# Scan stage of a two-layer metaformer: where ScalarE's steps stand between the recurrence steps, and which engine forms the last sum

## The chip, the cores and the metric

The kernel runs on one core of a Trainium2 chip. The metric is the device time of one launch in microseconds. The profile names the engines PE (TensorE, with PEld for its weight loads), DVE (VectorE), ACT (ScalarE), POOL (GpSimd) and SP (SyncE, which here only issues DMAs). All data is fp32.

## The reference, cut to what matters

Input x is 64 images of 56 x 56 tokens with 128 channels. Layer 0 is a window attention and a recurrent network, layer 1 a state-space convolution and a mixture of experts. The change touches the stage that holds layer 0's recurrence and layer 1's convolution:

```python
# layer 0, second half: 3136 dependent steps for all 64 images
yt = sigmoid(wx_t + yt @ Vt)
t = t + ys                                   # residual: input of layer 1
# layer 1, first half, per token of n = layernorm(t)
fg = sigmoid(n @ Wf + bf + 2); ig = sigmoid(n @ Wi + bi); delta = softplus(n @ Wd + bd) * 0.1
inp = delta * ig * (B * n)                   # complex product, B from a DFT of 7 x 7 taps
for _ in range(16):                          # h_r, h_i
    h = fg * (A * h) + inp                   # done in closed form, by repeated squaring
x3 = t + h                                   # the last sum of residual and convolution
```

## The kernel before, in words

`scan_phase` (lines 623 to 1265) is written with an explicit program for each engine and semaphores between them. Tokens are taken in NCH = 25 chunks of TF = 128 (the last has 64), images in NO = 4 groups of OS = 16. `slots()` (L744) yields pairs (j, s) of chunk and group. In one slot three things run side by side, each for another group:

* the recurrence of chunk j: K = 32 steps k. At each, PE multiplies the last state by `vh` (L1236) and ACT takes the tanh (L1107). PE then has to wait for ACT and ACT for PE, so every further instruction that either engine is given stands, in program order, between two steps.
* the front half for group `oc`: PE turns the states back to token-major and adds the input (`turn_u`, L1194: two 512-column passes of `ident` on `X2` and eight short ones), ACT evacuates this into `X2` (`residual`, L1073), DVE takes statistics (L910), POOL the inverse root (L832 to L836), ACT normalizes into `XN` (L1123), PE turns it (`turn_normal`, L1219), ACT evacuates it (L1142), and PE and ACT make 16 gates (L1265, L1084, L1086). At the slot's end ACT runs an Exp and a Ln over the whole group (L1164, L1166), each after a table load.
* the back half for group `o = oc - 1`: DVE's chain of products L986 to L1043, with seven squares by ACT in between (L1128 to L1157). DVE counts its steps in the semaphore `dv` (NV = 24 a group), ACT its squares in `am` (NA = 7). The last two DVE instructions are L1041 (half the sum of `Wv` and `IN`) and L1043 (`X2` added, result in `IN`), and SP stores `IN` (L794).

PE also turns the next chunk's inputs (`turn_inputs`, L1207) into bank `pX`, and ACT copies them to `XU` (`keep_turned`, L1061), with the state order changed in that copy: it reads 512 contiguous values and writes each to a place 256 bytes from the one before. Every eighth step PE adds `inputs` (L1191, 512 columns). `turn_u` for the next group stands at k = 24, 26, 28 and 30, except in slot s = 3; for s = 0 it stands at k = 0 to 3 of its own slot. The order of work is written out by hand: each engine's loop over k has the places in `if` conditions. Nothing is planned by a program.

SP loads `X2` of group o+1 (L781) once `dv` says that the group two before is finished, as there are NX = 3 buffers. The slot order on SP is load, DFT rows, store.

Of the kernel before, what the change touches and what calls it, by code (L numbers as in the profile page):

```python
# [14 lines left out]
ALU = mybir.AluOpType  # L15
# [607 lines left out]
def scan_phase(nc, B, x1_d, xh_d, gram, w_ffnT, v_ffnT, gamma, beta, w_gates, b_gates, dft, kernA, kernB,  # L623
# [7 lines left out]
    OS = 16  # L631
# [3 lines left out]
    NX = 3  # L635
# [6 lines left out]
    NV = 24  # L642
# [18 lines left out]
    with ExitStack() as ctx:  # L661
# [68 lines left out]
        dv = sem("dv"); am = sem("am")  # L730
# [13 lines left out]
        def slots():  # L744


            for j in range(-1, NCH + 2):
                for s in range(NO):
                    g = (j - 1) * NO + s
                    if g <= NGR:  # L750
                        yield (j, s, g if 0 <= g < NGR else None, g - 1 if 1 <= g else None,
                               0 <= j < NCH, j + 1 < NCH)
# [10 lines left out]
        def _(sp):  # L763
# [20 lines left out]
            for j, s, oc, o, scan, prep in slots():  # L784
                if oc is not None and oc + 1 < NGR:
                    load_x1(oc + 1)
# [4 lines left out]
                if o is not None:  # L791
                    c, s_ = divmod(o, NO)
                    sp.wait_ge(dv, o * NV + NV)
                    sp.dma_start(tokens(x3_d, OS * s_, OS, c),  # L794
                                 IN[0:size(c)].rearrange("t r b c -> t (r b c)").rearrange("t (b c) -> t b c", b=OS)
                                 ).then_inc(x3_st, 16)
# [3 lines left out]
        def _(pool):  # L800
# [14 lines left out]
            for j, s, oc, o, scan, prep in slots():  # L815
# [28 lines left out]
        def _(dve):  # L844
# [114 lines left out]
            for j, s, oc, o, scan, prep in slots():  # L959
# [6 lines left out]
                if o is not None:  # L966
# [32 lines left out]
                    wait(dve, x3_st, o * 16)  # L999
# [3 lines left out]
                if o is not None:  # L1003
                    after(7)
                    turned_by(tm, Wv, inp, a, wp_d, wv_d, o)
                    dve.wait_ge(am, o * NA + 3)
# [9 lines left out]
                if o is not None:  # L1016
                    dve.wait_ge(am, o * NA + 5)
# [3 lines left out]
                    did(dve.scalar_tensor_tensor(f1[:, 1], t1, -1.0, d1, ALU.add, ALU.mult))  # L1021
                    did(dve.scalar_tensor_tensor(f0[:, 0], f0[:, 0], -0.25, d0, ALU.add, ALU.add))
                    did(dve.scalar_tensor_tensor(t0, t0, 1.0, d0, ALU.add, ALU.mult))
                    dve.wait_ge(am, o * NA + 6)
# [25 lines left out]
        def _(act):  # L1050
# [10 lines left out]
            def keep_turned(j, s, q):  # L1061
# [5 lines left out]
                if j >= 1:  # L1067
                    act.wait_ge(y_ps, i - 2 * NO * NQ + 1)
                act.copy(XU[n % 2][:, 0:size(n), b0:b0 + Q].rearrange("c t b -> c b t"),
                         pX[:, 0:Q * size(n)].rearrange("c (b t) -> c b t", b=Q)).then_inc(xt_sb, 1)  # L1070
                load_xq(i + 2)

            def residual(oc, q):  # L1073
# [3 lines left out]
                act.copy(X2[oc % NX][0:tc, Q * q:Q * q + Q, :].rearrange("t b c -> t (b c)"), pY[0:tc, :]).then_inc(x2_d, 1)  # L1077

# [12 lines left out]
            for j, s, oc, o, scan, prep in slots():  # L1091
# [11 lines left out]
                for k in range(K):  # L1103
# [7 lines left out]
                    if conv and s + 1 < NO and k in (25, 27, 29, 31):  # L1111
                        residual(oc + 1, (k - 25) // 2)
                    if prep and k in (1, 4, 7, 10):
                        keep_turned(j, s, k // 3)
                    if conv and 10 <= k < 10 + NQ:
                        q = k - 10
                        if q == 0:
# [4 lines left out]
                        for i in range(Q * q, Q * q + Q):  # L1122
                            w = act.activation(XN[0:tc, i, :], X2[oc % NX][0:tc, i, :], ACT.Identity,  # L1123
                                               bias=nmr[0:tc, i:i + 1], scale=rst[0:tc, i:i + 1])
                        w.then_inc(xn_d, 1)
                    if o is not None and k == 6:
                        needs(4)
                        act.activation(t1, t0, ACT.Square).then_inc(am, 1)  # L1128
                        act.activation(f0[:, 0], t0, ACT.Square, bias=cols[0:tm, 1:2]).then_inc(am, 1)
                    if o is not None and k == 8:  # L1130
                        act.activation(d1, d0, ACT.Square).then_inc(am, 1)
                    if o is not None and k == 14:
                        act.wait_ge(am, o * NA + 3)
                        act.activation(d2, d1, ACT.Square).then_inc(am, 1)
                    if scan and s == NO - 2 and k == 25:
                        act.wait_ge(mag_d, j + 1)
                        act.activation(sc_[0:size(j)], sa[0:size(j)], ACT.Tanh, scale=0.5).then_inc(th_d, 1)
                    if conv and 12 <= k < 12 + NQ:
                        q = k - 12
# [7 lines left out]
                    if o is not None and k == 16:  # L1147
                        needs(8)
                        act.activation(t2, t1, ACT.Square).then_inc(am, 1)
                    if o is not None and k == 20:  # L1150
                        if conv:
                            act.wait_ge(bx_d, oc + 1)
                        act.activation(f1[:, 0], t1, ACT.Square, bias=cols[0:tm, 2:3]).then_inc(am, 1)
                    if o is not None and k == 22:
                        needs(11)
                        act.wait_ge(am, o * NA + 6)
                        act.activation(t1, t2, ACT.Square, bias=cols[0:tm, 2:3]).then_inc(am, 1)  # L1157
# [11 lines left out]
        def _(pe):  # L1169
# [36 lines left out]

            def turn_inputs(j, s, q, oc):  # L1207
# [7 lines left out]
                for b in range(Q):  # L1215
                    w = pe.transpose(pX[:, tn * b:tn * b + tn], XQ[i % 2][0:tn, b, :], ident[0:tn, 0:tn])
# [9 lines left out]
            for j, s, oc, o, scan, prep in slots():  # L1226
# [4 lines left out]
                for k in range(K):  # L1231
# [17 lines left out]
                    if conv and s + 1 < NO and k in (24, 26, 28, 30):  # L1249
                        turn_u(oc + 1, (k - 24) // 2)  # L1250
                    if prep and k in (0, 3, 6, 9):
                        turn_inputs(j, s, k // 3, oc)
                    if conv and 11 <= k < 11 + NQ:
                        if k == 11:
                            if scan and s == NO - 2:
                                pe.wait_ge(raw_d, j + 1)
                            if prep:
                                pe.wait_ge(xt_sb, ((j + 1) * NO + s) * NQ + NQ)
                        turn_normal(oc, tc, k - 11)
# [552 lines left out]
```

## Time and profile before

| | us |
|---|---|
| median of 3 runs | 14605.63 |
| lowest, highest | 14566.55, 14616.49 |
| the profiled execution, its span | 14537.58, 14535.8 |
| Exp of the first and of the last of 100 groups in the scan stage, start | 5509.7, 11648.4 |

The page also gives the busy share of the whole span: PE 79%, PEld 60%, DVE 76%, ACT 68%, POOL 28%. These are means over all stages. For this change only the stretch between the two Exp instructions matters, where DVE's digit in the 40 slices is 9 throughout and the granted TensorE clock is 6 to 7 tenths. A time in the rows is the start from the span's beginning, and the next number the duration of the group of instructions. An instruction's duration overlaps the next one's on the same engine, so what it costs in a queue is the distance from its start to the next start.

### The profile page before, as it was taken

What the parts mean: (1) busy time and instruction counts of PE and PEld (TensorE: products, weight loads), DVE (VectorE), ACT (ScalarE), POOL (GpSimd) and SP (SyncE); (2) the same over time, 40 slices, a digit from 0 to 9 for tenths busy, and PEclk for the clock granted to TensorE, in tenths of its full rate; (3) what the DMA queues carried; (4) which work ended last, traced back from release to release, by engine and by line L of the source; (5) the groups of instructions that cost most, each with busy time, mean ns of one, the idle gap of its engine ahead of it and who ended that gap; (6) DMA issues with size and microseconds to landing.
All of it is one profiled execution on the core that took longest, in us unless ns stands there. A gap on an engine that the chain in (4) does not pass through costs nothing. (4 is left out here: it accounts for less than half of the span.)

```text
span 14535.8 us, 248087 instructions
## 1 busy us (share of the span) xinstructions
PE 11419.5 (79%) x87538; PEld 8744.4 (60%) x87538; DVE 11053.6 (76%) x22880; ACT 9833.3 (68%) x22679; POOL 4012.8 (28%) x3975
## 2 busy tenths in 40 slices
PE   7888888888888867777777777777777547776998
PEld 5666666666666645555555555555555235555888
DVE  6777777777777718999999999999999965554133
ACT  6888888888888846666666666667666567776100
POOL 5444444445444421212111211112121111211000
PEclk9999999999999967777777777777777677777555
DMA  3333333333333321111111111111111133333599
GB/s 69 86 81 82 81 82 87 76 90 73 90 77 86 75 61 41 53 53 53 51 47 52 53 53 53 51 46 53 53 52 40 23 84 94 99 90 89 172 316 309
DMA packets 1967708, 1189.72 MB, mean 82 GB/s; under 512 B 48853, under 2 KB 1900056, under 8 KB 1958436
## 3 DMA queue, kind: packets, MB, share of 16 engines
q1 hardware_dynamic: 1554148, 967.87, 26.3%
q10 hardware_dynamic: 408832, 205.55, 5.0%
q8 instruction: 641, 10.50, 0.3%
q14 instruction: 439, 3.60, 0.1%
q0 software_dynamic: 3648, 2.20, 0.1%
HBM read 708.85 MB, written 466.62 MB: 81 GB/s over the span
## 5 line engine op out<-in xcount | busy, mean ns | idle before, releaser
L1236 PEld LDWEIGHTS s_pW<-s_XU,s_vh 128*128 128x128 f32 x6272 | 1415.7, 261 | 1969.1 <-ACT s_XU L1107 1699.7
L1236 PE MATMUL s_pW<-s_XU,s_vh 128*128 128x64 f32 x6272 | 1493.2, 331 | 1071.4 <-ACT s_XU L1107 1071.4
L1107 ACT ACTIVATE s_XU<-s_pW,s_zb 128x64 f32<-128x64 f32 x3136 | 995.7, 318 | 1788.7 <-PE s_pW L1236 1738.1
L1265 PE MATMUL s_pG<-s_wg,s_XNT 128*128 128x384 f32 (+1 forms) x3200 | 1506.0, 559 | 37.5 <-ACT s_Z L1086 37.5
L832 POOL TENSOR_TENSOR s_rst<-s_var,s_epst 128x16 f32<-128x16 f32 (+1 forms) x100 | 141.7, 1417 | 3906.6 <-DVE s_var L79 3906.6
L408 ACT ACTIVATE KB<-pV,qkb 32x392 f32<-32x392 f32 x2048 | 1190.5, 581 | 25.0 <-PE pV L498 1.1
L248 POOL TENSOR_TENSOR SS<-SS,mx 128x784 f32<-128x784 f32 x512 | 769.5, 1503 | 804.8 <-DVE mx L341 804.6
L1203 PEld LDWEIGHTS s_pY<-s_hident,s_XU 128*128 128x128 f32 (+1 forms) x3200 | 752.2, 305 | 177.7 <-issue 129.6
L1711 PE MATMUL c_pS<-c_OX,c_Wm 64*112 64x128 f32 x3584 | 737.6, 420 | 91.1 <-DVE c_X L1727 76.6
L460 ACT ACTIVATE XH<-XR,nm,rs 112x128 f32<-112x128 f32 x1792 | 733.6, 485 | 92.1 <-POOL nm L267 83.6
L506 PE MATMUL pS<-KB,QT 128*64 128x196 f32 x8192 | 793.7, 336 | 0.0
L1711 PEld LDWEIGHTS c_pS<-c_OX,c_Wm 64*112 64x112 f32 x3584 | 728.2, 304 | 100.5 <-DVE c_X L1727 85.7
L1123 ACT ACTIVATE s_f<-s_X,s_nmr,s_rst 128x128 f32<-128x128 f32 (+1 forms) x1600 | 658.0, 492 | 162.0 <-POOL s_nmr L836 161.9
L528 PE MATMUL pV<-wq,XT 128*49 128x64 f32 x16384 | 565.7, 222 | 251.0 <-ACT KB L408 250.7
L1453 ACT ACTIVATE r_Y<-r_X,r_nmr,r_rst 112x128 f32<-112x128 f32 x1792 | 718.7, 508 | 56.6 <-POOL r_nmr L1395 56.6
L506 PEld LDWEIGHTS pS<-KB,QT 128*64 128x64 f32 x8192 | 544.9, 137 | 352.6 <-issue 284.9
L256 POOL TENSOR_TENSOR XR<-XR,pbias 112x512 f32<-112x512 f32 x448 | 571.6, 1276 | 650.9 <-DMA XR<-in_x_dram 650.9
L352 DVE RECIPROCAL rc<-pO 128x16 f32<-128x16 f32 x512 | 131.3, 256 | 796.9 <-PE pO L549 796.9
L549 PE MATMUL pO<-Vb,PT 128*64 128x66 f32 x16384 | 591.1, 225 | 169.3 <-DVE gram L346 165.6
L1203 PE MATMUL s_pY<-s_hident,s_XU 128*128 128x128 f32 (+1 forms) x3200 | 716.8, 369 | 0.0
L528 PEld LDWEIGHTS pV<-wq,XT 128*49 128x49 f32 x16384 | 490.1, 124 | 371.4 <-ACT KB L408 370.9
L1727 DVE TENSOR_TENSOR c_X<-c_pS,c_X 112x512 f32<-112x512 f32 x448 | 307.4, 691 | 521.6 <-PE c_pS L1711 391.4
(249 smaller groups left out, 31958.3 us busy)
## 6 DMA issues: line engine op xcount, KB each, us to landing
XL<-in_x_dram SPq DMA_DIRECT2D x64, 1568.0 KB, 12.4
XR<-in_x_dram SPq DMA_DIRECT2D x64, 1568.0 KB, 18.0
x_dram<-XR SPq DMA_DIRECT2D x64, 1568.0 KB, 8.1
xh_dram<-XH SPq DMA_DIRECT2D x64, 1568.0 KB, 8.1
r_X<-x_dram SPq DMA_DIRECT2D x64, 1568.0 KB, 14.2
c_X<-x_dram SPq DMA_DIRECT2D x64, 1568.0 KB, 19.4
out_dram<-c_X ACTq DMA_DIRECT2D x64, 1568.0 KB, 13.9
s_XQ<-xh_dram ACTq DMA_DIRECT2D x384, 256.0 KB, 2.8
```

Of the source, the lines that this page charges most:

```text
L248: pool.tensor_tensor(sv[:], sv[:], mx[wi % 2][:].unsqueeze(2).broadcast_to([P, 16, L]), ALU.subtract).then_inc(s_sub, 1)
L408: i = act.activation(KB[par][r, :, h, :], pV[r, 0:NW * L].rearrange("c (w l) -> c w l", l=L), ACT.Identity, bias=qkb[r, 1:2])
L460: i = act.activation(XH[q.par][:, n0, 0:C], XR[q.par][:, n0, :], ACT.Identity, bias=nm2[:, k, t:t + 1], scale=rs2[:, k, t:t + 1])
L506: i = pe.matmul(pS[64 * s:64 * s + 64, p // 2, (p % 2) * NH * L:(p % 2 + 1) * NH * L], QT[par][:, w * L:w * L + 64], KB[par][:, w, :, :].r ...
L528: i = pe.matmul(pV[64 * o:64 * o + L, 64 * w:64 * w + 64], XT[im.par][:, wi, w, :], wq[:, 2 * C:3 * C].rearrange("c (a b d) -> c a b d", a ...
L1107: act.activation(XU[j % 2][:, t, :], pW[t // R % 2][:, B * (t % R):B * (t % R) + B], ACT.Tanh, bias=zb[:, 0:1], scale=0.5).then_inc(u_sb, 1)
L1123: w = act.activation(XN[0:tc, i, :], X2[oc % NX][0:tc, i, :], ACT.Identity, bias=nmr[0:tc, i:i + 1], scale=rst[0:tc, i:i + 1])
L1203: w = pe.matmul(pY[0:tc, C * i:C * i + C], XU[c % 2][:, 0:tc, OS * s + Q * q + i], hident[:], start=False, stop=True, skip_group_check=True)
L1236: pe.matmul(pW[t // R % 2][:, B * (t % R):B * (t % R) + B], vh[:], before, start=False, stop=True, skip_group_check=True).then_inc(z_ps, 1)
L1265: pe.matmul(pG[i % 3][0:tc, 0:3 * C], XNT[:, i, 0:tc], wg[:], start=True, stop=True).then_inc(g_ps, 1)
L1453: w = act.activation(Y[m.par][o][:, t, :], X[m.par][o][:, t, :], ACT.Identity, bias=nmr[m.par][o][:, t:t + 1], scale=rst[m.par][o][:, t:t ...
L1711: w = pe.matmul(bank[0:T, C * t:C * t + C], Wm[m.par][E * o:E * o + E, T * n:T * n + T], OX[m.par][E * o:E * o + E, :], start=True, stop=True)
```

## The change

1. The last sum. DVE's L1041 becomes a plain sum of `Wv` and `IN`, L1043 goes, NV is 23. In the next slot PE adds `X2` and `Wv` in bank `pN` (`last_sum`, two matmuls of 512 columns by `ident`, a quarter of the group at k = 1, 3, 5 and 7), and ACT evacuates each quarter into `X2` at k = 2, 4, 6 and 8, with the constant 0.5 as bias. SP stores `X2` after ACT's four, and only then reloads that buffer for the group three later; in the slot the load stands last now.
2. ACT's places. The normalization runs two rows at a step over eight steps from k = 7 (k = 11 for s = 0), where it ran four at a step over four steps from k = 10. The evacuations that follow come at every second step. The squares move from k = 6, 6, 8, 14, 16, 20, 22 to 6, 15, 17, 19, 21, 22, 24, in another order, and DVE's waits on `am` are renumbered. The residual's turn moves to k = 17, 19, 21, 24, its copies to 18, 20, 22, 25. The inputs' turns are at 0, 2, 4, 7, their copies at 1, 3, 5, 8.
3. The inputs' order. `turn_inputs` writes `pX` with a step of four values, and `keep_turned` reads it contiguously and writes four adjacent values at a time.

```diff
-    NV = 24
+    NV = 23
+        TURN_IN = (0, 2, 4, 7)
+        KEEP_IN = (1, 3, 5, 8)
+        TURN_U = (17, 19, 21, 24)
+        KEEP_U = (18, 20, 22, 25)
+        def normal_at(s):
+            return 11 if s == 0 else 7
...
             def load_x1(o):
-                wait(sp, dv, (o - NX + 1) * NV)
+                wait(sp, x3_st, (o - NX + 1) * 16)
...
+                    sp.wait_ge(f_sb, f * NQ + NQ)
+                    sp.dma_start(tokens(x3_d, OS * s_, OS, c), X2[f % NX][0:size(c)]).then_inc(x3_st, 16)
+                if oc is not None and oc + 1 < NGR:
+                    load_x1(oc + 1)
...
+                    wait(dve, f_ps, o * NQ)
                     turned_by(tm, Wv, inp, a, wp_d, wv_d, o)
...
-                    did(dve.scalar_tensor_tensor(flat(wv), flat(wv), 0.5, flat(inp), ALU.add, ALU.add))
-                    after(23)
-                    did(dve.tensor_tensor(flat(inp).rearrange("t (b r c) -> t b r c", b=OS, r=2),
-                                          X2[o % NX][0:tm].rearrange("t b (r c) -> t b r c", r=2),
-                                          wv.rearrange("t r b c -> t b r c"), ALU.add))
+                    did(dve.tensor_tensor(flat(wv), flat(wv), flat(inp), ALU.add))
...
-                act.copy(XU[n % 2][:, 0:size(n), b0:b0 + Q].rearrange("c t b -> c b t"),
-                         pX[:, 0:Q * size(n)].rearrange("c (b t) -> c b t", b=Q)).then_inc(xt_sb, 1)
+                act.copy(XU[n % 2][:, 0:size(n), b0:b0 + Q],
+                         pX[:, 0:Q * size(n)].rearrange("c (t b) -> c t b", b=Q)).then_inc(xt_sb, 1)
...
+            def last_sum(f, q):                                   # ACT
+                act.wait_ge(f_ps, f * NQ + q + 1)
+                act.activation(X2[f % NX][0:tf_, Q * q:Q * q + Q, :]..., pN[0:tf_, :],
+                               ACT.Identity, bias=cols[0:tf_, 1:2]).then_inc(f_sb, 1)
...
-                    if conv and 10 <= k < 10 + NQ:                # normalization, 4 rows at a step
+                    i = 2 * (k - normal_at(s))
+                    if conv and 0 <= i < OS:                      # 2 rows at a step
...
-                    if conv and 12 <= k < 12 + NQ:                # evacuation of the turned rows
+                    if conv and k - normal_at(s) - 3 in (0, 2, 4, 6):
...
+                        if k == 24:
+                            needs(11)
+                            act.wait_ge(am, o * NA + 5)
+                            act.activation(t1, t2, ACT.Square, bias=cols[0:tm, 2:3]).then_inc(am, 1)
...
+            def last_sum(f, q):                                   # PE
+                wait(pe, f_sb, f * NQ + q)
+                pe.matmul(pN[0:tf_, :], ident[0:tf_, 0:tf_], X2[f % NX][0:tf_, Q * q:Q * q + Q, :]..., start=True, stop=False)
+                pe.matmul(pN[0:tf_, :], ident[0:tf_, 0:tf_], Wv[0:tf_, :, Q * q:Q * q + Q, :]..., start=False, stop=True
+                          ).then_inc(f_ps, 1)
...
-                    w = pe.transpose(pX[:, tn * b:tn * b + tn], XQ[i % 2][0:tn, b, :], ident[0:tn, 0:tn])
+                    w = pe.transpose(pX[:, 0:Q * tn].rearrange("c (t b) -> c t b", b=Q)[:, :, b], XQ[i % 2][0:tn, b, :],
+                                     ident[0:tn, 0:tn])
...
+                    if f is not None and k in (1, 3, 5, 7):
+                        if k == 1:
+                            pe.wait_ge(dv, f * NV + NV)
+                        last_sum(f, k // 2)
```

## Rows read from the trace of the kernel before

**Rows 1.** Busy time in one round of four slots (columns: engines, granted clock, DMA).

```profile
7816.57:8065.75 249.18, 186.40 (x707) 134.74 (x706) 236.83 (x223) 171.39 (x413) 44.08 (x18) 0.75 0.19 51
```

**Rows 2.** Timeline of ACT, the Exp at three slot ends; then all Exp instructions.

```profile
7878.06 1.91 ACT L1164 ACTIVATE s_Dl<-s_Z 128x2048 f32<-128x2048 f32 x1
...
7927.75 1.92 ACT L1164 ACTIVATE s_Dl<-s_Z 128x2048 f32<-128x2048 f32 x1
...
8004.28 1.91 ACT L1164 ACTIVATE s_Dl<-s_Z 128x2048 f32<-128x2048 f32 x1
...
L1164 ACT ACTIVATE s_Dl<-s_Z x100: 1910/1912/1922, 5509.7 to 11648.4; 128x2048 f32<-128x2048 f32 x96, 64x2048 f32<-64x2048 f32 x4
```

**Rows 3.** Waits in the same round (waiter, releaser: us in total, times, longest).

```profile
ACT s_XU L1107 <- PE s_pW L1236: 69.3, 49, 3.5
...
DVE s_BX L905 <- ACT s_f L1123: 8.5, 3, 5.4
...
ACT s_f L1123 <- POOL s_nmr L836: 5.9, 1, 5.9
```

**Rows 4.** Timeline of ACT in slot s = 1 (tanh k = 0, 1, 7, 15, 16, 24, 25).

```profile
8010.82 0.31 ACT L1107 ACTIVATE s_XU<-s_pW,s_zb 128x64 f32<-128x64 f32 x1
...
8011.91 0.31 ACT L1107 ACTIVATE s_XU<-s_pW,s_zb 128x64 f32<-128x64 f32 x1 [0.78 <-PE s_pW L1236]
...
8018.71 1.05 ACT L1128 ACTIVATE s_t<-s_f 128x1024 f32<-128x1024 f32 x1
...
8020.69 0.30 ACT L1107 ACTIVATE s_XU<-s_pW,s_zb 128x64 f32<-128x64 f32 x1
...
8024.26 1.04 ACT L1069 COPY s_XU<-s_pX 128x512 f32<-128x512 f32 x1
...
8025.07 1.64 ACT L1123 ACTIVATE s_f<-s_X,s_nmr,s_rst 128x128 f32<-128x128 f32 x4
...
8034.10 0.71 ACT L1142 ACTIVATE s_XNT<-s_pN,s_cols 128x512 f32<-128x512 f32 x1
...
8034.68 0.33 ACT L1107 ACTIVATE s_XU<-s_pW,s_zb 128x64 f32<-128x64 f32 x1
...
8035.78 0.32 ACT L1107 ACTIVATE s_XU<-s_pW,s_zb 128x64 f32<-128x64 f32 x1 [0.20 <-PE s_pW L1236]
...
8046.64 0.31 ACT L1107 ACTIVATE s_XU<-s_pW,s_zb 128x64 f32<-128x64 f32 x1
...
8050.01 0.32 ACT L1107 ACTIVATE s_XU<-s_pW,s_zb 128x64 f32<-128x64 f32 x1 [2.63 <-PE s_pW L1236]
```

**Rows 5.** Timeline of PE, a residual's turn at the low clock and at the high.

```profile
7936.23 2.07 PE L1200 MATMUL s_pY<-s_X,s_ident 128*128 128x512 f32 x2 [0.88 <-ACT s_X L1077]
7938.09 1.84 PE L1203 MATMUL s_pY<-s_hident,s_XU 128*128 128x128 f32 x8
...
7984.97 1.08 PE L1200 MATMUL s_pY<-s_X,s_ident 128*128 128x512 f32 x2
7985.89 1.81 PE L1203 MATMUL s_pY<-s_hident,s_XU 128*128 128x128 f32 x8
```

**Rows 6.** Timeline of DVE in slot s = 1.

```profile
8008.71 1.23 DVE L986 TENSOR_TENSOR s_f<-s_TG 128x1024 f32<-128x1024 f32 x1
...
8045.50 1.23 DVE L1027 SCALAR_TENSOR_TENSOR s_t<-s_t,s_d 128x1024 f32<-128x1024 f32 x1 [0.46 <-ACT s_t L1157]
...
8063.93 2.29 DVE L1043 TENSOR_TENSOR s_IN<-s_X,s_Wv 128x2048 f32<-128x2048 f32 x1
```

**Rows 7.** Windows of one us in slot s = 0 (the number after POOL is the granted clock).

```profile
7939.00:7940.00 1.00, 1.00 (x8) 1.00 (x8) 0.97 (x1) 0.00 (x0) 0.00 (x0) 0.69 0.00 0
...
7949.00:7950.00 1.00, 0.01 (x1) 0.00 (x0) 0.97 (x2) 1.00 (x2) 0.00 (x0) 0.93 0.37 99
```

**Rows 8.** DMA issues of the round (KB each, median us from issue to landing).

```profile
x_dram<-s_IN SPq DMA_DIRECT2D x4, 1024.0 KB, 5.9
...
s_X<-x_dram SPq DMA_DIRECT2D x4, 0.5 KB, 8.8
```

More of the change, by code:

```diff
@@ L779, in load_x1 @@
                 c, s = divmod(o, NO)
-                wait(sp, dv, (o - NX + 1) * NV)
+                wait(sp, x3_st, (o - NX + 1) * 16)
                 sp.dma_start(X2[o % NX][0:size(c)], tokens(x1_d, OS * s, OS, c)).then_inc(x2_ld[o % NX], 16)
             load_x1(0)
-            for j, s, oc, o, scan, prep in slots():
-                if oc is not None and oc + 1 < NGR:
-                    load_x1(oc + 1)
+            for j, s, oc, o, f, scan, prep in slots():
                 if scan and s == 1:
@@ L813, in _ @@
             pool.tensor_tensor(fld[4], fld[3], nhalf[:, 0:C], ALU.pow).then_inc(pch, 1)
-            for j, s, oc, o, scan, prep in slots():
+            for j, s, oc, o, f, scan, prep in slots():
                 if scan and s == NO - 2:
@@ L957, in bounded @@
                 dve.wait_ge(pa_d, b0 + 8)
-            for j, s, oc, o, scan, prep in slots():
+            for j, s, oc, o, f, scan, prep in slots():
                 if scan and s == NO - 2:
@@ L1089, in _ @@
                 load_xq(i)
-            for j, s, oc, o, scan, prep in slots():
+            for j, s, oc, o, f, scan, prep in slots():
                 conv = oc is not None
@@ L1110, in _ @@
                         residual(oc, k - 1)
[L1111 to L1114, printed above, removed]
-                    if conv and 10 <= k < 10 + NQ:
-                        q = k - 10
-                        if q == 0:
+                    if conv and s + 1 < NO and k in KEEP_U:
+                        residual(oc + 1, KEEP_U.index(k))
+                    if f is not None and k in (2, 4, 6, 8):
+                        last_sum(f, k // 2 - 1)
+                    if prep and k in KEEP_IN:
+                        keep_turned(j, s, KEEP_IN.index(k))
+                    i = 2 * (k - normal_at(s))
+                    if conv and 0 <= i < OS:
+                        if i == 0:
                             act.wait_ge(rs_d, oc + 1)
@@ L1121, in _ @@
                             wait(act, n_ps, oc * NQ)
-                        for i in range(Q * q, Q * q + Q):
+                        for i in (i, i + 1):
                             w = act.activation(XN[0:tc, i, :], X2[oc % NX][0:tc, i, :], ACT.Identity,
                                                bias=nmr[0:tc, i:i + 1], scale=rst[0:tc, i:i + 1])
[L1125 to L1137, printed above, removed]
-                    if conv and 12 <= k < 12 + NQ:
-                        q = k - 12
+                        if i % Q == Q - 1:
+                            w.then_inc(xn_d, 1)
+                    if conv and k - normal_at(s) - 3 in (0, 2, 4, 6):
+                        q = (k - normal_at(s) - 3) // 2
                         act.wait_ge(n_ps, oc * NQ + q + 1)
@@ L1205, in turn_u @@
                 w.then_inc(y_ps, 1)
+            def last_sum(f, q):
+                c = f // NO
+                tf_ = size(c)
+                wait(pe, f_sb, f * NQ + q)
+                pe.matmul(pN[0:tf_, :], ident[0:tf_, 0:tf_], X2[f % NX][0:tf_, Q * q:Q * q + Q, :].rearrange("t b c -> t (b c)"),
+                          start=True, stop=False, skip_group_check=True)
+                pe.matmul(pN[0:tf_, :], ident[0:tf_, 0:tf_], Wv[0:tf_, :, Q * q:Q * q + Q, :].rearrange("t r b c -> t b r c"),
+                          start=False, stop=True, skip_group_check=True).then_inc(f_ps, 1)
             def turn_inputs(j, s, q, oc):
@@ L1224, in turn_normal @@
                 w.then_inc(n_ps, 1)
-            for j, s, oc, o, scan, prep in slots():
+            for j, s, oc, o, f, scan, prep in slots():
                 conv = oc is not None
```

81 lines of the change are left out of this document (49 added, 32 removed).

## The prediction, made before the changed kernel had run

> **What bounds the kernel now.** The page's 40 slices come first: between the two Exp instructions DVE has its 9 in every slice, and everything else is lower. That looks like a DVE-bound stage, and it nearly is: in a round of four slots DVE is busy 236.8 of 249.2 us [rows 1]. The waits tell more. DVE stands 8.5 us a round for ACT's normalization; ACT waits for DVE's side once a round, 5.9 us through POOL's scale in slot s = 0, and otherwise only for PE, 69.3 us in 49 waits [rows 3]. So two chains run side by side and are almost equally long: DVE's (236.8 of work, some 10 of waits) and the recurrence's, PE and ACT in turns (243.3 of its own, 5.9 of waits). In slots s = 1, 2 and 3 no wait of the recurrence's on DVE is seen: there it sets the time by itself. The Exp starts give the slots' lengths: s = 2 61.5 us, s = 3 49.7 (no residual's turn at its end), s = 0 76.5, s = 1 61.5 [rows 1, 2].
>
> Then the timeline of slot s = 1. From Exp to the first tanh, with two table loads and the Ln, 6.5 us; a step with nothing else 1.09; sixteen steps from k = 0 to 16 take 24.96; 16 to 24 take 10.86; from 24 to the next Exp 19.1, as each turn of a residual makes its step 3.37 [rows 1, 2, 4]. PE's clock is at the low level (1.2 GHz, granted 0.5) for the first half of a slot and at the high one later. In slot s = 0 a dense run of turns started at 7936.2 and the clock rose within 7939 to 7940; it fell within 7949 to 7950, after the run had ended [rows 5, 7].
>
> **The change part by part.** I go through the steps of each slot with the durations of the rows. What an instruction costs in the queue: tanh 0.2, a 512-column evacuation 0.57, a 1024-element square about 1.0, a copy of turned inputs 0.8, two normalized rows 0.8 (four: 1.64) [rows 4]. A 512-column pass costs PE 1.86 at the low clock and 0.92 at the high one [rows 5].
>
> (a) *DVE*: one instruction of 2.29 less a slot [rows 6], 9.2 a round. This is worth time only where DVE sets the pace, which it does for 5.9 us a round.
>
> (b) *PE's last sum*: eight 512-column passes a slot, four pairs. They can't hide: behind the recurrence's matmul a plain step leaves PE about 0.7 us, and a pair needs 1.8 at the high clock or 3.6 at the low. The steps k = 3 and 5 come to 2.0 and 2.2 in place of 1.1 (the second and later pairs also start after ACT's evacuation of the one before, 0.5 after the tanh's neighbour is issued). The first pair, k = 1, falls into the low clock, as PE had stood over 6 us during Exp and Ln. It also has a new wait, for DVE's last instruction of the group before. Queued behind that wait on PE are all later matmuls, the recurrence's first, and for these ACT. When is DVE done? Its tail from L1027 to L1041's end is 63.93 - 45.50 = 18.4 us [rows 6], and L1027 needs the last square, which the change puts from k = 22 to k = 24. From k = 24 to the Exp are now 11.0 us, as the turns are earlier. So DVE ends at 1.35 + 18.4 - 11.0 = 8.8 us after the Exp, where PE would be ready at 7.2: a stall of 1.7 us a slot. Step k = 1: 1.7 + 3.6 = 5.3 instead of 1.1.
>
> (c) *ACT's places*. Before, k = 10 to 15 carried 16 rows, four evacuations, a copy and a square: the steps 10 to 15 took 11.7 of the 24.96. Spread two rows at a time they fit in or near the 1.1 step. By my list the steps 0 to 15 are now 1.1, 5.3, 1.5, 2.0, 0.9, 2.2, 1.7, 1.75, 2.4, 1.1, 2.1, 1.2, 1.55, 1.2, 1.55, 1.2: 28.7 us, 3.7 more. In it the clock rises during k = 1 and is down again by k = 9, since from there on PE has only short work; k = 10 holds a 512-column pass at the low clock (2.1). From k = 16 to the Exp: 1.7, 4.45 (the first turn meets the rest of the low clock), 1.75, 3.4, 1.1, 3.4, 2.0, 0.9, 3.4, 1.1, 1.75, four of 0.87, 1.3: 29.6 against 30.0. Three squares are hidden behind turns, one isn't. Slot s = 1: 6.5 + 28.7 + 29.6 = 64.7, 3.2 more. s = 2: 0.5 more again, since PE waits for the spectrum copy as well: 65.2, 3.7 more.
>
> (d) *s = 3* has no turns behind which the five squares at k = 17 to 24 could hide, and two more of them now stand there: +1.6, and about 0.8 for DVE's product that ACT's square at k = 21 needs. With +4.0 from the first half: 56.1, 6.4 more. *s = 0*: the 5.9 us of waiting are filled, four pairs cost about 7.6 (the clock is up by then), spread squares and rows give some 3 back: 75.2, 1.3 less. The normalization ends at k = 18 there, and DVE's product after it just reaches ACT at k = 21.
>
> Round: +3.2 + 3.7 + 6.4 - 1.3 = +12.0. There are (11648.4 - 5509.7) / 249.2 = 24.6 rounds [rows 1, 2]: +296. At the stage's end the last group is summed with nothing beside it: four pairs in turns with ACT, about 14, less DVE's 2.3: +12. Sum +308: 14,845 for an execution like the profiled one (14,537.6 us). That execution was 68 us below the median of the three runs, and I add the same to the median: 14,606 + 308 = about 14,910.
>
> (e) *DMA*. The store, 5.9 us to landing, now has to end before the load, 8.8 (measured with the store beside it) [rows 8]. The last quarter is in place at about 24 us after the Exp and the turn that needs the load stands at 36.8: 24 + 5.9 + 6.7 to 8.8 = 36.6 to 38.7, so 0 to 2 us of stall. I take 0, since alone the load should be quicker, and keep the 2 for the range.
>
> (f) *Inputs' order*. A copy with scattered writes costs 0.8, an evacuation of equal size with contiguous ones 0.57 [rows 4]. The new copy lies between; only at k = 8 is it on the path: 0 to -0.25 a slot, taken as 0. What PE's scattered write costs no row shows; bounds are nothing, and as much again as the turn takes (0.9 a slot on the path).
>
> The Trainium skill, page "SBUF — State Buffer", in its note on cachelines, says that SBUF works in lines of 16 bytes and PSUM in lines of 8, and that any non-contiguous access of PSUM slows matmuls down significantly. By it the copy would gain all of its 0.25, for it writes whole lines now, and the four turns a slot would lose. The trace has no matmul that writes with a step, so it doesn't say. By the rule the sum would be larger than mine, toward the third rival.
>
> **Rivals.**
> 1. *DVE sets the pace* (ends faster). If the pairs at k = 1, 3, 5, 7 hid in the recurrence's gaps, the recurrence's chain would stay below DVE's, and each slot would lose DVE's 2.29: 9.2 x 24.6 = 226, less the 12 at the end: 14,390. For it speaks DVE's 95%. Against it: the gap in a step is 0.7 and the pair 1.8. It decides if the steps 0 to 15 take under about 23 us.
> 2. *The clock stays high* from k = 2 on through k = 17. PE has eight more dense passes in the first half. Then the pass at k = 10, the short turns, the first gate and the first turn lose 3.0 us a slot, 12 a round, which is the whole loss: 14,606 + 12 = 14,620, with some 60 on both sides. Against it: at 7949 the clock fell although tanh and recurrence went on [rows 7].
> 3. *More is lost*: the load is late and the scattered turns are slow. 1.5 us a slot more, 6 a round: 15,060.
>
> **How the numbers follow.** Forecast (14,750 to 15,060 as its own range) 0.53, rival 1 0.13, rival 2 0.22, rival 3 0.12. Within 0.3%, about what a measurement can tell from no change here, is 14,562 to 14,649: half of rival 2 and the forecast's edge, 0.12. Faster: rival 1, a quarter of rival 2, and 0.04 from steps that I made too long: 0.22. Slower: 0.66. The range 14,450 to 15,120 leaves rival 1 out below and a little of rival 3 above.
>
> **What would show it.** The distance of the Exp instructions: 64.7, 65.2, 56.1, 75.2. PE's wait at k = 1 for DVE's L1041 of some 1.7 us in each slot. DVE idle ahead of L1027, about 5 us a slot for the last square, instead of 0.4. The granted clock at the high level from about 12 to 25 us after the Exp, low until about 39. The ACT wait on POOL in slot 0 under 1 us. The forecast is wrong if the first sixteen steps are below 25 us, or if DVE's idle share is not above a tenth.

## The result, and the profile after

| | before | after |
|---|---|---|
| median (lowest to highest), us | 14605.63 (14566.55 to 14616.49) | 14831.82 (14828.02 to 14870.7) |
| profiled execution, us | 14537.58 | 14831.82 |

The ratio is 1.017 [1.013, 1.021]: slower by 226 us by the medians, by 294 by the profiled executions. Those 294 come apart at four marks of the traces: the first Exp is 14.4 us earlier, from the first Exp to the last it is 6371.7 in place of 6138.7 (+233.0), from the last Exp to the next stage's first load 90.1 in place of 71.3 (+18.8), and that stage, whose code is the same, takes 1728.4 in place of 1677.0 (+51.4). About 5 us are left for all the rest. The profiled execution of before was quicker than every other execution of it on record (14,546 to 14,637 us), so the medians are the fairer pair for the total.

The round of four slots after, by the columns of [rows 1] (busy time of PE, PEld, DVE, ACT and POOL with counts, granted clock, DMA share, GB/s):

```profile
8002.24:8261.95 259.71, 204.77 (x771) 133.68 (x770) 227.81 (x219) 175.33 (x429) 40.21 (x18) 0.86 0.18 49
```

DVE has 9 us less to do, as intended, and PE 18 more, though its clock is up from 0.75 to 0.86. No engine is busy all the time, and the round is 10.5 longer. Its Exps, timeline of ACT, to be set against [rows 2]:

```profile
8075.52 1.91 ACT L1180 ACTIVATE s_Dl<-s_Z 128x2048 f32<-128x2048 f32 x1
...
8141.62 1.91 ACT L1180 ACTIVATE s_Dl<-s_Z 128x2048 f32<-128x2048 f32 x1
```

The others start at 8002.24 (the end of s = 3), 8205.94 and 8261.95. The slots of this round, and in the last two columns their means over the 21 rounds of groups 9 to 92, from the Exp starts of the trace:

| slot | before | predicted | after | before, mean | after, mean |
|---|---|---|---|---|---|
| s = 1 | 61.5 | 64.7 | 66.1 | 61.5 | 64.0 |
| s = 2 | 61.5 | 65.2 | 64.3 | 61.5 | 65.0 |
| s = 3 | 49.7 | 56.1 | 56.0 | 49.7 | 56.4 |
| s = 0 | 76.5 | 75.2 | 73.3 | 76.3 | 73.6 |

The slot s = 1 of this round, whose timeline is shown below, is one of two that took 66.1; all others in these rounds took 62.8 to 65.0. The mean round went from 248.9 to 258.8 us.

Who waits for whom in that round (waiter, releaser: us in total, times, longest), against [rows 3]:

```profile
ACT s_XU L1118 <- PE s_pW L1262: 79.1, 47, 6.0
...
DVE s_t L1035 <- ACT s_t L1170: 10.2, 3, 5.0
...
DVE s_BX L912 <- ACT s_f L1136: 9.7, 1, 9.7
PEld s_pN L1227 <- DVE s_Wv L1049: 5.7, 3, 2.2
...
DVE s_f L1033 <- ACT s_f L1163: 3.7, 2, 2.1
...
DVE s_f L1030 <- ACT s_f L1159: 2.3, 1, 2.3
```

The recurrence's wait on PE grew by 10, DVE now stands in three places for ACT's squares (before 0.46 at the last one [rows 6]), PE's new waits on DVE's last sum are there, and ACT's wait on POOL in slot 0 is gone. Slot s = 1 in PE's timeline shows the new wait and the pair behind it (a start, a duration, and in brackets the idle time with its releaser, the instruction whose end let it start):

```profile
8082.42 0.69 PE L1262 MATMUL s_pW<-s_XU,s_vh 128*128 128x64 f32 x2 [6.90 <-ACT s_XU L1118]
8084.64 2.08 PE L1227 MATMUL s_pN<-s_X,s_ident 128*128 128x512 f32 x2 [1.53 <-DVE s_Wv L1049]
8086.51 1.91 PE L1229 MATMUL s_pN<-s_Wv,s_ident 128*128 128x512 f32 x2
8088.21 0.53 PE L1262 MATMUL s_pW<-s_XU,s_vh 128*128 128x64 f32 x2
...
8090.35 0.85 PE L1241 MATMUL s_pX<-s_ident,s_XQ 128*128 128x128 f32 x4
...
8093.15 0.61 PE L1241 MATMUL s_pX<-s_ident,s_XQ 128*128 128x128 f32 x4
```

And ACT's in the same slot (tanh k = 1, the copy of turned inputs, tanh k = 2, 3, 16, 17, 18):

```profile
8083.15 0.31 ACT L1118 ACTIVATE s_XU<-s_pW,s_zb 128x64 f32<-128x64 f32 x1 [0.78 <-PE s_pW L1262]
...
8083.36 0.58 ACT L1073 COPY s_XU<-s_pX 128x512 f32<-128x512 f32 x1
8088.78 0.31 ACT L1118 ACTIVATE s_XU<-s_pW,s_zb 128x64 f32<-128x64 f32 x1 [4.84 <-PE s_pW L1262]
...
8091.41 0.31 ACT L1118 ACTIVATE s_XU<-s_pW,s_zb 128x64 f32<-128x64 f32 x1 [1.74 <-PE s_pW L1262]
...
8110.98 0.33 ACT L1118 ACTIVATE s_XU<-s_pW,s_zb 128x64 f32<-128x64 f32 x1
...
8112.64 0.31 ACT L1118 ACTIVATE s_XU<-s_pW,s_zb 128x64 f32<-128x64 f32 x1 [0.76 <-PE s_pW L1262]
8118.44 0.31 ACT L1118 ACTIVATE s_XU<-s_pW,s_zb 128x64 f32<-128x64 f32 x1 [4.11 <-PE s_pW L1262]
```

Step k = 1, the distance from one tanh to the next, is 5.63 long where a plain step is 1.09. DVE's tail in the same slot, against [rows 6]:

```profile
8082.29 2.29 DVE L1049 TENSOR_TENSOR s_Wv<-s_Wv,s_IN 128x2048 f32<-128x2048 f32 x1
...
8126.05 1.23 DVE L1033 SCALAR_TENSOR_TENSOR s_f<-s_f,s_d 128x1024 f32<-128x1024 f32 x1 [2.14 <-ACT s_f L1163]
8132.30 1.23 DVE L1035 SCALAR_TENSOR_TENSOR s_t<-s_t,s_d 128x1024 f32<-128x1024 f32 x1 [5.02 <-ACT s_t L1170]
```

L1035 needs the last square, as L1027 did before. It starts 9.3 us ahead of the Exp that ends the slot (8141.62), where L1027 started 20.3 ahead (8045.50, Exp at 8065.75). Its tail behind it is as long as before less one instruction, so DVE's last instruction of a group now ends 9.1 us behind the Exp, where it ended 0.5 behind. The last square stands two steps later, and all four turns of the residual now stand ahead of it or in its step.

### The profile page after: what moved, and what is told of

It is laid out like the page before. It is cut to its first block and busy times, and to the rows that moved or that the text cites. A ratio compares the mean times of both kernels' runs of the same rounds, so it can differ in the third digit from the quotient of the medians.

```text
span 14830.0 us, 251778 instructions
## 1 busy us (share of the span) xinstructions
PE 11976.7 (81%) x89138; PEld 8804.3 (59%) x89138; DVE 10825.2 (73%) x22780; ACT 9928.5 (67%) x23079; POOL 3911.3 (26%) x3975
## 5 line engine op out<-in xcount | busy, mean ns | idle before, releaser
L1262 PEld LDWEIGHTS s_pW<-s_XU,s_vh 128*128 128x128 f32 x6272 | 1228.3, 223 | 1854.9 <-ACT s_XU L1118 1460.8
L1262 PE MATMUL s_pW<-s_XU,s_vh 128*128 128x64 f32 x6272 | 1320.6, 298 | 904.6 <-ACT s_XU L1118 898.0
L1304 PE MATMUL s_pG<-s_wg,s_XNT 128*128 128x384 f32 (+1 forms) x3200 | 1468.0, 546 | 6.5 <-ACT s_Z L1097 6.5
L839 POOL TENSOR_TENSOR s_rst<-s_var,s_epst 128x16 f32<-128x16 f32 (+1 forms) x100 | 90.9, 909 | 4161.7 <-DVE s_var L79 4161.7
L1227 PE MATMUL s_pN<-s_X,s_ident 128*128 128x512 f32 (+1 forms) x800 | 536.8, 758 | 301.6 <-DVE s_Wv L1049 184.5
L1136 ACT ACTIVATE s_f<-s_X,s_nmr,s_rst 128x128 f32<-128x128 f32 (+1 forms) x1600 | 697.3, 489 | 8.9 <-POOL s_nmr L843 8.9
## 6 DMA issues: line engine op xcount, KB each, us to landing
s_XQ<-xh_dram ACTq DMA_DIRECT2D x384, 256.0 KB, 2.8
```

Of the source, the lines that this page charges most:

```text
L1262: pe.matmul(pW[t // R % 2][:, B * (t % R):B * (t % R) + B], vh[:], before, start=False, stop=True, skip_group_check=True).then_inc(z_ps, 1)
L1304: pe.matmul(pG[i % 3][0:tc, 0:3 * C], XNT[:, i, 0:tc], wg[:], start=True, stop=True).then_inc(g_ps, 1)
```

## The experiments

Twelve kernels, in the order in which they ran. "Scan" is the distance from the first Exp to the last (before 6138.7, after 6371.7), "next stage" the stage behind it (before 1677.0, after 1728.4). Slots are s = 1, 2, 3, 0 of one round; "mean round" is the mean over the 21 rounds of groups 9 to 92 (before 248.9, after 258.8), and the safer number, as single slots differ from their means by up to 2.1 us. The ratio is to executions of before that ran beside the run; their medians were 14,555 to 14,611, so medians of different rows are better compared by the ratio or the scan.

| run | median us | ratio to before [95%] | scan | slots | mean round | next stage |
|---|---|---|---|---|---|---|
| e1_spread_only | 14830.5 | 1.0185 [1.0168, 1.0202] | 6407.5 | 63.8, 64.0, 58.3, 71.9 | 260.0 | 1756.1 |
| e2_sum_only | 14934.0 | 1.0256 [1.0239, 1.0273] | 6507.4 | 67.6, 66.3, 55.3, 77.0 | 265.7 | 1687.8 |
| e3_early_square | 14729.7 | 1.0111 [1.0094, 1.0128] | 6286.2 | 62.8, 61.7, 56.7, 74.8 | 255.2 | 1754.3 |
| e4_one_pass | 14624.4 | 1.0049 [1.0033, 1.0066] | 6215.2 | 60.8, 63.2, 56.0, 72.3 | 252.5 | 1697.9 |
| e5_spread_early | 14758.5 | 1.0099 [1.0072, 1.0126] | 6299.9 | 61.8, 62.4, 57.7, 74.0 | 255.6 | 1754.1 |
| e6_gap_fill | 14809.2 | 1.0145 [1.0121, 1.0169] | 6326.1 | 62.7, 62.4, 56.0, 75.1 | 257.0 | 1743.1 |
| e7_early_fill | 14659.5 | 1.0032 [1.0020, 1.0044] | 6200.0 | 60.4, 60.3, 54.6, 74.0 | 251.6 | 1743.9 |
| e8_early_gap_fill | 14718.2 | 1.0075 [1.0052, 1.0098] | 6237.6 | 60.6, 61.4, 55.4, 75.1 | 253.4 | 1756.6 |
| e9_slot0_rows | 14847.7 | 1.0182 [1.0164, 1.0201] | 6376.0 | 63.5, 64.6, 56.0, 73.1 | 259.1 | 1704.9 |
| e10_fill_rows | 14616.6 | 1.0018 [1.0008, 1.0028] | 6145.4 | 60.3, 59.8, 55.7, 73.5 | 249.3 | 1747.6 |
| e11_fill_rows_sq | 14557.2 | 0.9971 [0.9960, 0.9983] | 6085.7 | 59.6, 59.5, 55.1, 72.8 | 247.4 | 1756.0 |
| e12_before_fill | 14480.0 | 0.9934 [0.9918, 0.9951] | 6034.1 | 58.7, 59.8, 48.0, 78.6 | 244.4 | 1718.5 |

### Which part costs what

e1 keeps the new places and undoes the sum, with SP's store and load as before; e2 is the kernel before with the sum alone; e3 is the kernel after with the last squares earlier; e4 halves PE's part of the sum and so leaves the convolution out of the result. The edits are cut to what matters.

```diff
# e1, against after
-    NV = 23
+    NV = 24
-    dve.tensor_tensor(flat(wv), flat(wv), flat(inp), ALU.add)
+    dve.scalar_tensor_tensor(flat(wv), flat(wv), 0.5, flat(inp), ALU.add, ALU.add)
+    dve.tensor_tensor(IN, X2, Wv, ALU.add)
-    if f is not None and k in (1, 3, 5, 7): last_sum(f, k // 2)        # PE
-    if f is not None and k in (2, 4, 6, 8): last_sum(f, k // 2 - 1)    # ACT
# e2, against before: the same lines the other way round
# e3, against after
-    if k == 22:      # square d2
+    if k == 21:
-    if k == 24:      # last square, t1
+    if k == 22:
# e4, against after, in PE's last_sum
-    pe.matmul(pN[0:tf_, :], ident, X2[...], start=True, stop=False)
-    pe.matmul(pN[0:tf_, :], ident, Wv[...], start=False, stop=True)
+    pe.matmul(pN[0:tf_, :], ident, X2[...], start=True, stop=True)
```

**e1.** 

> The changed kernel without its last sum on PE: DVE keeps both last instructions, as before, ACT's places and the inputs' order are those of the change. My theory (PE's pairs lengthen the recurrence's chain, the spread shortens it): the sixteen steps 0 to 15 come to about 21.3 us, slots s = 1 and 2 would need 57 us, DVE with 59 us a slot sets the pace, round 241 to 245 us, time 14,400 to 14,480. Rival (it is the new places and orders of ACT's work that cost, the pairs are hidden in the gaps): slower than before, 14,700 or more.

A miss, and the one that taught most: the new places alone are as slow as the whole change. The rival's time held, but not its reason, as e2 shows that the pairs are not hidden. Waits of its round:

```profile
ACT s_t L1156 <- DVE s_d L1000: 18.3, 3, 7.1
...
ACT s_f L1140 <- POOL s_nmr L845: 10.4, 4, 7.4
DVE s_t L1037 <- ACT s_t L1174: 9.2, 3, 5.0
```

With no pairs the first steps are short, so ACT reaches its first square (L1156, k = 6) before DVE has made the product for it. DVE is late there because its tail started late, behind the last square at k = 24 (L1037 waits for L1174), and behind L1156 stand all later tanhs. In the mean DVE's last instruction ends 11.4 us behind the Exp in s = 1 and 2, where before it was 0.5. That is a ring over two slots: late square, DVE's tail, first products, first square, the rest of the recurrence, late square. The timeline has it once:

```profile
7857.85 1.06 ACT L1156 ACTIVATE s_t<-s_f 128x1024 f32<-128x1024 f32 x1 [5.47 <-DVE s_d L1000]
```

**e2.** 

> The kernel before with only the last sum moved to PE and ACT (pairs at k = 1, 3, 5, 7, evacuations at 2, 4, 6, 8), all other places as before. My theory: no stall at k = 1, as DVE ends before the Exp there, but each pair lengthens its step: +5.5 us in slots 1, 2 and 3, about 0 in slot 0, where the wait on POOL is filled; round 265, time about 15,000. Rival (pairs hidden, DVE's 2.29 us a slot is gained): 14,390. Rival (the stall for DVE's last instruction at k = 1 is what costs): 14,600.

A hit in the round, 266 us, and nearly in the time (14,934 for 15,000). Besides the pairs themselves DVE now waits for PE to have read `Wv`:

```profile
DVE s_Wv L903 <- PE s_pN L1216: 17.8, 4, 6.5
```

Places and sum alone cost 269 and 369 us of the scan, together 233. They don't add up. With the new places DVE's end is on the ring, so there the saved instruction of 2.29 us is worth time, and the sum on PE makes the scan 36 us shorter (after against e1), where with the old places it makes it 369 longer. The pairs and the late DVE cover each other in the kernel after: while PE works at the pairs, ACT does not have to wait at its first square. e4 below shows this once, in s = 3; for the other slots it is the reading that fits.

**e3.** 

> The changed kernel with ACT's last two squares earlier (k = 21 and 22 in place of 22 and 24), nothing else. My theory: DVE ends some 2.4 us earlier in each slot, the PE stall at k = 1 of 1.5 us goes in all four slots, round 254 to 256, time 14,690 to 14,740. Rival (the stall is cover for something else, the load or the clock, and comes back there): within 0.3% of the changed kernel, 14,790 to 14,880.

Right in the round (256.0) and in the time. PE's wait at k = 1 on the last sum is no longer among the round's waits, and DVE's for the last square is down from 10.2 to 5.2:

```profile
DVE s_t L1035 <- ACT s_t L1170: 5.2, 2, 2.6
```

So the stall in s = 1, 2 and 3 comes from the place of the last squares, and that is worth 86 us of the scan.

**e4.** 

> The changed kernel without the second matmul of each last-sum pair: the convolution is missing from the sum, all waits stay. It prices one 512-column pass in four steps. My theory: 1.8 us at the low clock and three times 0.9 at the high one are on the recurrence's path, 4.4 a slot where DVE doesn't take over: round 244 to 248, time 14,460 to 14,560. Rival (the pairs are mostly hidden behind ACT): less than 1 us a slot, 14,750 or more.

The direction was right and the size was not: the round fell by 7.4, not by 12 to 16, and the time of 14,624 is above the expected 14,460 to 14,560. PE's wait for DVE at k = 1 stayed (5.9), DVE's for the last square too (9.5): with half of the pairs gone the ring is next. Slot s = 3 did not get shorter at all (mean 56.4 in both): there ACT now waits 2.4 us for DVE at its first square (L1152), which it did not in the kernel after. The four passes taken out are worth 156 us of the scan, and with the other four left the scan stays 77 above before.

### The places and the early squares without the sum

e5 is e1 with e3's two lines.

**e5.** 

> e1_spread_only with the last two squares at k = 21 and 22, as in e3. In e1 ACT stood 5.5 us at k = 6 for DVE, and DVE 5 us at L1037 for the square at k = 24: a ring of last square, DVE's tail (20.7 us), statistics, first products, square at k = 6. Theory formed after e1 (this ring and not the spread made e1 slow): 2.5 to 2.9 us off every slot, round 243 to 248, time 14,480 to 14,600. Rival (the spread places or the copies' new order cost by themselves): above 14,750.

A miss again: the round is 255.6 in the mean, not 243 to 248, and the time is the rival's. The earlier squares gave back 108 us of e1's 269. Slots 1 and 2 are then within a us of before. What stays, 161 us of the scan, is in s = 3, 7.9 longer than before in the mean, less 3.0 in s = 0. ACT still waits 12.2 for DVE at its first square and 9.4 for POOL, and DVE still ends 8.9 us behind the Exp in s = 1 and 2: of a shift of 11 the two lines took back 2.5. The rest fits the residual's turns: three of them still stand ahead of the last square, where all four stood behind it. No run moved the turns back, so this is argued and not shown. PE also waits for the next inputs in e5, 15.2 us in the round, a wait that neither before nor after has:

```profile
7887.49 1.11 PE L1245 MATMUL s_pX<-s_ident,s_XQ 128*128 128x128 f32 x4 [5.51 <-DMA s_XQ<-xh_dram]
```

In most slots this load is there before ACT's square is done, and the wait costs nothing by itself; in this one (s = 1) the turn started 0.9 us behind the square's end.

Set against e3, e5 also prices the sum with the new places and early squares: 6286.2 with the sum on PE, 6299.9 with it on DVE. There the exchange is about even.

### The clock

PE stands through Exp and Ln, and the first pair falls into the low clock. e6 gives PE idle matmuls there; e8 is e3 with the same; e7 has more of them in the thin steps.

```diff
# e6, against after; fill(n) is a matmul of ident by n columns into a free gate bank
+    if scan and oc and k == 0:
+        wait(pe, g_sb, oc * OS - 2)
+        for _ in range(9):
+            fill(3 * C)
     if f is not None and k in (1, 3, 5, 7):
         if k == 1:
+            fill(3 * C)
             pe.wait_ge(dv, f * NV + NV)
# e8: e3 and e6.   e7: e8, and
+    if scan and oc and k in (9, 11, 12, 13, 14, 15):
+        fill(2 * C)
```

**e6.** 

> The changed kernel with idle matmuls on PE while ACT does Exp and Ln: nine of 384 columns at k = 0 and one at k = 1, into a free bank, results unused. PE has nothing to do there, so they cost nothing by themselves. Theory (the low clock at k = 1 and 2 costs 1.8 + 1.1 us a slot, on the path): round 247 to 250, time 14,530 to 14,620. Rival (these steps are covered by DVE's ring through the late square, the clock is not the matter): within 0.3% of the changed kernel.

PE's timeline of slot s = 1: the first pair now takes 1.8 us, not 3.6.

```profile
7802.61 1.13 PE L1227 MATMUL s_pN<-s_X,s_ident 128*128 128x512 f32 x2 [1.08 <-DVE s_Wv L1049]
7803.57 1.02 PE L1229 MATMUL s_pN<-s_Wv,s_ident 128*128 128x512 f32 x2
7804.43 0.33 PE L1265 MATMUL s_pW<-s_XU,s_vh 128*128 128x64 f32 x2
```

In the mean slots 1 and 2 gained 1.1 and 2.2, while s = 3 and s = 0 lost 0.5 and 0.7: 46 us of the scan, less than expected, and the time is within 0.3% of the changed kernel's, as the rival had it. DVE's last instruction ends 9.1 us behind the Exp, as in the kernel after, so the first pair starts no sooner, and only its own time is won. The clock also fell again earlier, within 7817 to 7820, some 24 us behind the Exp where the kernel after has 27. The idle matmuls cost something too. In s = 0 they start only behind a turn of the residual and end behind the first tanh; the step from k = 0 to k = 1 takes 2.9 in place of 1.1 in all kernels that have them. The row is from e12 below, where that tanh started at 7891.47:

```profile
7888.17 5.97 PE L1220 MATMUL s_pG<-s_wg,s_ident 128*128 128x384 f32 x18
```

**e8.** 

> e3_early_square with the idle matmuls of e6 only. Theory: e3's and e6's gains add: round 243 to 246, time 14,420 to 14,500, under the kernel before. Rival (both shorten the same wait at k = 1): no more than the better of e3 and e6, 14,600 or above.

**e7.** 

> e3_early_square with the idle matmuls of e6 and six more of 256 columns at k = 9 and 11 to 15, to keep the clock at its high level through the first gates. Theory: 2.9 us a slot as in e6, 2.5 more from k = 10, 16 and 17, until DVE with 57 us of work and its waits takes over: round 238 to 243, time 14,290 to 14,450. Rival (the matmuls of the middle lengthen the steps by what they bring): equal to e8, within 0.3%.

e8 gained 49 us of the scan over e3, e7 another 38. With e7 the granted clock of the round is 0.98, so next to nothing is left to win by the clock, and this round is still 249.3, the mean one 251.6. Both were expected well faster than before and were not; e8 came out as its rival had it, e7 0.4% below e8 and far from its forecast. s = 3 and s = 0 together took 131.1 in the mean of e7 (before 126.0), and the next stage took 67 us (e7) and 80 (e8) more than in the profile of before.

### Slot 0, and the squares once more

e9 normalizes four rows at a step in slot 0 only, from k = 10; e10 is e7 with that; e11 has two squares one step earlier as well.

```diff
# e9, against after (places of the turns and their evacuations in s = 0 moved with it)
-    i = 2 * (k - normal_at(s))
+    i = 2 * (k - 7) if s else 4 * (k - 10)
# e11, against e10: squares f1 and t1
-    if k == 21:
+    if k == 20:
-    if k == 22:
+    if k == 21:
```

**e9.** 

> The changed kernel, but in slot s = 0 the normalization is as before: four rows at a step from k = 10, the turned rows' evacuations at k = 12 to 15. In the changed kernel DVE stands 9.7 us there for the last row at k = 18 (5.4 before). Theory (this late end of the rows makes DVE late in s = 0, and by it the next slots): slots 3 and 0 together from 129.3 to 124 to 127 us, time 14,690 to 14,780. Rival (the rows are paid for by ACT's chain either way, DVE's wait is slack): within 0.3% of the changed kernel.

No gain: scan 6376.0 against 6371.7. DVE's 9.7 us of waiting for slot 0's normalization are down to 0.2, and its wait for the last square is up from 10.2 to 15.1 in the round: in the kernel after, the first of the two is slack.

**e10.** 

> e7_early_fill (earlier squares, idle matmuls) with the four rows at a step in slot 0 of e9. In e7 slots 1 and 2 take 60.4 each, below the 61.5 of before, but 3 and 0 take 128.6 against 126.2. Theory: these two come to 121 to 125, round 242 to 246, time 60 to 200 us under the kernel before of the same chip, ratio 0.986 to 0.996. Rival (DVE's wait in slot 0 is slack): ratio 1.00 to 1.005 as in e7.

**e11.** 

> e10 with the squares for L1033 and L1035 one step earlier still (k = 20, 21 and 21), the latter two behind a turn on PE. Theory (DVE's remaining 2.6 us waits for the last square are on its ring): 1 to 2 us a slot less than e10 where DVE paces, ratio to e10 0.990 to 0.997. Rival (the recurrence's chain paces by now): equal to e10, or slower, as k = 20 has a square more and no turn to hide it.

On top of e7 the same rows are worth 55 us of the scan, far less than e10 expected, and its ratio of 1.0018 is within the rival's. The earlier squares are worth 60 more, as e11 expected. With 6085.7 the scan of e11 is below the one of before by 53, and its whole time by 0.3% [0.2, 0.4].

```profile
7788.03:8035.03 247.00, 220.88 (x901) 145.03 (x900) 227.99 (x219) 175.27 (x429) 40.21 (x18) 0.97 0.19 52
```

### Does the change have a part in that gain?

e12 is the kernel before with idle matmuls and nothing else.

```diff
# e12, against before
+    if scan and oc and k == 0:
+        wait(pe, g_sb, oc * OS - 2)
+        for _ in range(9):
+            fill(3 * C)
+    if scan and oc and k in (1, 4, 5, 7, 8, 10, 15):
+        fill(2 * C)
```

**e12.** 

> The kernel before with idle matmuls on PE only (nine of 384 columns after the turned inputs of k = 0, beside Exp and Ln, and one of 256 columns at k = 1, 4, 5, 7, 8, 10, 15). Theory 'clock alone': all that e11 won over before comes from the clock; then before gains as much from the same matmuls, 10 us a round and 200 or more in all: 14,350 to 14,420. Theory 'DVE paces before': slots 1 and 2 are filled by DVE's products (busy 95% of the round), PE's clock is not what they wait for; slots 1 and 2 stay at 61 to 62, slots 3 and 0 at 126 to 128 together, the time between 14,560 and 14,660, and e11's gain needs the DVE product that the change took away together with the fill and the earlier squares.

Between the two expectations, and the fastest of all: 0.66% below before [0.5, 0.8], where e11 is 0.29% below. Its round:

```profile
7777.10:8022.21 245.11, 203.31 (x836) 139.96 (x835) 236.68 (x223) 171.01 (x413) 44.08 (x18) 0.91 0.19 52
```

"DVE paces before" was too strong: slots 1 and 2 fell from 61.5 to 59.0 and 59.1 in the mean, so PE's clock had been a part of them. s = 3 gained 1.2, and s = 0 lost 1.4. "The clock alone" was too strong too: at 245.1 DVE is busy for 236.7, and only 8.4 are left. So e11's gain needs nothing of the change: with idle matmuls in both, the kernel without the change has a scan 52 us shorter than the best form of the change.

## Why the prediction was right, and where its sizes were off

**Right by its own mechanism.** The pairs don't hide (e2, e4), and with the old places DVE's saved instruction is worth nothing (e2). Steps 0 to 15 of slot s = 1 took 28.9 us (8082.05 to 8110.98), 28.5 in the mean, forecast 28.7; k = 1 took 5.6, forecast 5.3; DVE ended its tail at 8082.29 + 2.29, 9.1 us after the Exp, forecast 8.8; it stood 5.0 ahead of L1035 for the last square, forecast "about 5", though in s = 1 and 2 only. The wait on POOL in slot 0 is gone. DVE's idle share of the round is 31.9 of 259.7, above the tenth.

**Sizes.** (b) PE's stall was 1.5 us in s = 1, and 5.7 in the round's three waits of the weight load, forecast 1.7 a slot: right, except that s = 0 has none. (c) From k = 17 to 18, the first turn, 5.80 instead of 4.45, since the clock was low for nearly the whole of it. This is the long slot of 66.1: over the 21 slots s = 1 the step took 4.1 in the mean, a little under the forecast. (The forecast counts three squares behind turns and one not; of the five at k = 17 to 24 four stand with a turn. Its list of steps is not touched by that.) The forecast had the clock high from 12 to 25 us after the Exp and low until 39. Here it was high from 15 on, until 32, and low until about 43; in most other slots s = 1 it was high from 14 to 27 and low until 38:

```profile
8089.00:8090.00 1.00, 1.00 (x2) 0.23 (x1) 1.00 (x2) 0.67 (x2) 0.92 (x2) 0.50 0.00 0
...
8092.00:8093.00 1.00, 1.00 (x4) 0.40 (x3) 1.00 (x2) 0.20 (x1) 1.00 (x1) 1.00 0.27 73
8106.00:8107.00 1.00, 0.51 (x3) 0.38 (x4) 1.00 (x2) 1.00 (x4) 0.00 (x0) 1.00 0.07 22
8108.00:8109.00 1.00, 0.55 (x4) 0.36 (x3) 1.00 (x2) 1.00 (x5) 0.00 (x0) 0.50 0.76 88
```

(d) s = 3 was met (56.0), s = 0 was 1.9 shorter than forecast. That s = 3 was met is no proof of its terms: 4.0 of the 6.4 were put down to the first half, where the pairs are, but s = 3 is 56.4 in the mean with half of the passes gone (e4) and 57.6 with none of them (e5). Over 24.6 rounds all this is +233 in place of +296. (e) The DMA: the load alone lands in 6.3 us (8.8 beside the store before [rows 8]), and PE waited for it 1.9 in the round: the lower end.

**Not in the prediction at all.** The stage behind, +51 between the two profiles without a change in its code. Against an execution like the profiled one (14,845) the sum was only 14 too high, because errors cancelled: the scan 63 less and the first Exp 14 earlier, against 51 in the next stage, 7 in the tail (18.8, forecast 12) and the 5 left over. The other 64 of the 78 by which 14,910 missed are the offset between profiled execution and median, added once from before, where after has none. By the medians the sum was 82 too high, 308 for 226, and 70 of these are the scan, the first Exp and the tail.

**What it did not see** is how the parts stand to each other. By its list of steps the kernel after without the pairs would be quick; it was expected at 14,400 to 14,480 (e1) and took 14,830. DVE's instruction, priced at next to nothing in (a), is worth time once DVE's end is on the ring. So the total is right because the list followed the one chain that the change as a whole makes, with the late DVE in it. As an account of which part costs what, it was wrong by 269 us: the later last square and the earlier turns put the end of DVE's tail of 18.4 us behind the next slot's start, which e1 shows as a wait of ACT and the kernel after as a wait of PE. The square's part of this is 108 us in e1 and 86 in the kernel after.

**(f) The inputs' order.** The copy with four adjacent values takes 0.58 where the scattered one took 1.04 [rows 4]; in the queue 0.47 in place of 0.81, a gain of 0.34, where I had priced 0 to 0.25. The copy at k = 8 of the slot above, with what follows it on ACT:

```profile
8100.83 0.58 ACT L1073 COPY s_XU<-s_pX 128x512 f32<-128x512 f32 x1
8101.30 0.89 ACT L1136 ACTIVATE s_f<-s_X,s_nmr,s_rst 128x128 f32<-128x128 f32 x2
```

PE's turn, which now writes with a step of four values, takes 0.61 at the high clock (the row at 8093.15 above). The same turn in the kernel before, which writes contiguously, from PE's timeline there:

```profile
7947.40 0.60 PE L1216 MATMUL s_pX<-s_ident,s_XQ 128*128 128x128 f32 x4
```

So the step cost nothing; over all turns of the inputs at the high clock the median is 0.60 in both kernels. The Trainium skill, page "SBUF — State Buffer", in its note on cachelines, has both halves of this: whole lines are cheaper, which the copy bears out, and non-contiguous access of PSUM slows matmuls down significantly, which these transposes don't bear out, at least for a write of this step. Here the measurement decides.

## What to carry to other kernels

An engine busy for 95% of a stage is not by that what sets its pace: compute the length of the other chain, and ask what waits for the instruction that is to be saved. When a step is moved later, add the length of everything that hangs on it across the loop's edge, and count what was put ahead of it as well; a move of two steps was worth 86 to 108 us of 14,600 here, more than most of the instructions argued about. And before work is given to an engine that idles, try what idle work on it does to the kernel as it is: here that was the better change, though it costs time wherever the idle work outlasts the gap.

## What the runs showed of the hardware that was not expected

The next stage's length differed though its code never did, and always with its granted clock. Windows over the whole of it, of the kernel before, and then of the kernel after:

```profile
11719.70:13396.70 1677.00, 1198.06 (x7168) 878.43 (x7168) 888.14 (x2624) 1206.56 (x2626) 338.94 (x192) 0.75 0.38 93
```

```profile
11957.10:13685.50 1728.40, 1253.13 (x7168) 922.29 (x7168) 887.00 (x2624) 1206.00 (x2626) 338.67 (x192) 0.72 0.36 91
```

DVE, ACT and POOL do the same work in the same time; PE's busy time is up by 55 us. Over the 14 profiles this stage took from 1677 to 1756 us. Whether it is the kernel ahead of it or the single execution that picks the length was not settled: each kernel has one profile, and all of them but the one of before lie at 1688 or above. Much speaks for the execution. The 52 executions of the kernel before beside the experiments took from 14,546 to 14,637 us, the quick ones at a granted clock of 0.809 over the whole execution and the slowest at 0.803; the profiled one had 14,538 at 0.810. One kernel thus varies by as much as this stage does over all kernels, and by the medians the change costs no more than its scan and tail. So the +51 may be no effect of the change. It is a sixth of the 294 us between the two profiles, so comparisons of the scan are better made by the Exp distances than by the total.
